# A pre-norm attention and LoRA block on one core: key parts written straight into their rows, x of the second chunk by tiles, the first layer norm in halves, 22 turns ahead of the first tile

## The chip, the cores and the metric

The kernel runs on 1 core of one Trainium2 chip. The metric is the device time of one execution in microseconds. Before the change the median of 3 runs is 701.74 us (701.54 to 702.16).

## What is computed

The input x has 2 x 1024 tokens of 512 numbers, all in float32. A block of attention is followed by a feed-forward block, each behind a layer norm without weights and each added back:

```python
x = x + attn(layernorm(x), Wqkv, Wo)     # 32 heads of 16, one key and value head shared by all, causal, ALiBi
x = x + ffn(layernorm(x), W_base, b_base, W_gate, A, B)   # x @ W_base.T + b + routed LoRA, top 2 of 8 experts
# attn: scores = q @ k.T * scale + slopes * (pos_k - pos_q), causal, softmax, @ v, heads joined, @ Wo
```

## The kernel before, in words

**Stages.** The tokens are four chunks of 512 (`c` = 0 to 3, two per batch). Ahead of the attention, chunk by chunk: SP loads x, VectorE makes the layer norm's statistics (`statistics`) and, with a first guess of the inverse deviation from ScalarE (`rstd_first`) and one Newton step, the normed x (`normalised`). TensorE turns it by 128x128 pieces (`turn_tile`, L663), ScalarE copies the turned tile out of PSUM (`copy_tile`, L887), and TensorE projects in float32 to queries (four groups of 128 columns) and to one group of 112 columns: six copies of the 16 key columns, and the values (`project`, L678).

**Parts.** The scores are made in bf16 matmuls from operands that hold a float32 number as a sum of bf16 parts: high, middle, low. Six products of parts are added by one matmul, since each stands in 16 rows of its own: `PARTS` says for each 16 rows which part of q and which of k stand there. For queries ScalarE makes the float32 copy and the high part (L899, L907), VectorE (queries 0 and 1) or POOL (the others) the rest, and SP writes the parts to DRAM (`store_queries`) and reads them back row group by row group (`load_queries`, six transfers). For keys ScalarE copies the group of 112 rows to `kv` (`keys_values`, L915); VectorE's `split_keys` makes the parts of all 96 rows in seven instructions (L1102 to L1114), the last three of which mask each part by a column of 0 and 1 and add them into `k_op`.

**Attention.** A step k handles one unit of 4 heads x 2 chunks of queries. Its maxima go one step ahead of its scores: TensorE fills a PSUM bank (`max_slot`, L732), VectorE takes the maximum out of it (L1145 on the diagonal, L1150 beside it): 40 such slots and 2 turns of the results per step, in three banks. Then come the scores (L759, L762), their exponentials by ScalarE (L965), and the product with the values (L780). 16 steps are followed by the output projection (L808) and the feed-forward block.

**Order.** Each engine runs a fixed list. TensorE's is made by `pe_order`: scores and values of the step before, slots of this step, and projections put among them (`AMONG`). A slot goes in where `slot_due` says, which spreads the slots by VectorE's time as `vector_time` guesses it: so many ns a slot, and 620 ns more for a slot that has a piece of `split_keys` behind it (`KEY_SLOTS`: seven slots in steps 0, 2 and 4, one for each piece). In step 0, chunk 1's keys are split behind slots 2 to 8; slots 16 on read `q_in[1]`, the second chunk's queries.

**What the change touches:** `PARTS`, `KEY_SLOTS` and `vector_time`; on SP the load of chunk 1's x (L455); on TensorE the start (L855); on ScalarE `rstd_first` (L878) and `keys_values` (L909); on VectorE `statistics` (L1068), `normalised` (L1083), `split_keys` (L1098) and the first calls (L1157).

## Time and profile before

| what | value |
|---|---|
| median of 3 runs | 701.74 us |
| the profiled execution's own time | 700.96 us |
| its span, first to last instruction | 699.2 us |
| TensorE busy (matmul) | 669.7 us, 96% |
| VectorE busy | 557.4 us, 80% |
| ScalarE busy | 358.6 us, 51% |
| POOL busy | 216.9 us, 31% |
| TensorE's share of the chain that ended last | 83% |

TensorE's busy time is close to the span, so what can be gained without less matmul work is the 29.5 us in which it stands still. A table by stretches shows where these lie.

### The profile page before, as it was taken

Reading aid. Unit: us, or ns where it says so; the run is one execution under the profiler, and the core shown is the slowest. Engines: PE = TensorE matmul, PEld = TensorE weight load, DVE = VectorE, ACT = ScalarE, POOL = GpSimd, SP = SyncE. Lnnn points to the kernel's source line nnn. Section 1 sums busy time; section 2 is a strip of 40 time slices with the busy share of each in tenths; the row PEclk is TensorE's granted clock in tenths of the full one; section 3 lists DMA queues with packets and bytes.
Section 4 is the critical chain, followed back from the end, with each engine's and each line's share of the span. In section 5 each row is a group of like instructions: output and inputs, shape, how many; then the busy total and the mean of one; then the engine's idle time right before and its main releaser. Section 6 shows DMA issues by size and latency. Waiting matters only on the chain.

```text
span 699.2 us, 13261 instructions
## 1 busy us (share of the span) xinstructions
PE 669.7 (96%) x4304; PEld 305.5 (44%) x4304; DVE 557.4 (80%) x1801; ACT 358.6 (51%) x511; POOL 216.9 (31%) x366
## 2 busy tenths in 40 slices
PE   3889999999999999999999999999999999999997
PEld 2434344544344444444443343433433455555553
DVE  5899889887989889898988989899881365666565
ACT  2324647567556676666666666767667411111111
POOL 0035424233332515243352231422432412222220
PEclk9999999999999999999999999999999999999999
DMA  8578108080411443080144744225200189700001
GB/s 253 130 145 137 64 2 136 30 147 28 166 54 51 60 89 108 11 131 34 41 63 94 102 81 77 49 49 94 48 18 33 52 130 170 162 30 30 31 30 60
DMA packets 42951, 56.32 MB, mean 81 GB/s; under 512 B 6648, under 2 KB 26232, under 8 KB 42752
## 3 DMA queue, kind: packets, MB, share of 16 engines
q1 hardware_dynamic: 40296, 51.27, 37.3%
q10 hardware_dynamic: 2592, 4.26, 1.8%
q8 instruction: 33, 0.54, 0.3%
q14 instruction: 30, 0.25, 0.1%
HBM read 35.72 MB, written 19.79 MB: 79 GB/s over the span
## 4 chain that ended last, share of the span: by engine, by line
PE 83%; DVE 10%; DMA 3%; ACT 2%; issue 1%; SPq 1%; POOL 0%; DVEq 0%; ACTq 0%; POOLq 0%
PE psum L780 20%; PE psum L732 18%; PE psum L762 13%; PE psum L808 8%; PE psum L830 7%; PE psum L678 7%; PE psum L759 5%; DVE psum L1145 3%; PE psum L825 2%; PE psum L840 2%; ACT work L965 2%; DMA x_sb<-in_x 1%; DVE negm L1150 1%; PE psum L817 1%; DMA arena<-q_dram 1%
## 5 line engine op out<-in xcount | busy, mean ns | idle before, releaser
L965 ACT ACTIVATE work<-psum 128x1024 f32<-128x1024 f32 (+1 forms) x320 | 289.0, 943 | 127.6 <-PE psum L762 108.5
L1145 DVE CUSTOM_DVE_ANT_0 psum<-psum,future 128x384 f32<-128x384 f32 (+3 forms) x512 | 237.7, 514 | 12.6 <-PE psum L732 10.4
L732 PE MATMUL psum<-k_op,arena 106*128 106x512 bf16 (+3 forms) x768 | 212.4, 328 | 9.6 <-DVE negm L1145 4.3
L1150 DVE TENSOR_REDUCE negm<-psum 128x1 f32<-128x512 f32 x256 | 168.6, 687 | 15.3 <-PE psum L732 10.9
L1318 POOL TENSOR_SCALAR_AFFINE_SELECT work<-work 128x512 f32<-128x512 f32 x128 | 81.2, 634 | 296.2 <-ACT work L965 296.2
L780 PE MATMUL psum<-work,v_op 128*32 128x512 f32 (+3 forms) x1536 | 163.5, 498 | 0.5 <-POOL work L1318 0.4
L762 PE MATMUL psum<-arena,k_op 109*128 109x512 bf16 (+3 forms) x640 | 157.3, 316 | 1.9 <-ACT work L965 0.8
L732 PEld LDWEIGHTS psum<-k_op,arena 106*128 106x128 bf16 x768 | 69.0, 97 | 128.5 <-DVE negm L1145 40.7
L678 PE MATMUL psum<-arena,wqkv_sb 128*128 128x256 f32 (+3 forms) x240 | 84.6, 453 | 1.1 <-ACT arena L887 1.1
L759 PE MATMUL psum<-arena,k_op 116*128 116x128 bf16 x512 | 84.3, 221 | 0.9 <-ACT work L965 0.9
L762 PEld LDWEIGHTS psum<-arena,k_op 109*128 109x128 bf16 x640 | 59.6, 98 | 44.5 <-ACT work L965 15.7
L1145 DVE DVE_READ_ACCUMULATOR2_ANT negm<- 128x1 f32 x512 | 70.0, 137 | 0.0
L759 PEld LDWEIGHTS psum<-arena,k_op 116*128 116x128 bf16 x512 | 44.4, 98 | 48.4 <-ACT work L965 36.1
L808 PE MATMUL psum<-wo_sb,wqkv_sb 128*128 128x512 f32 x128 | 59.0, 596 | 0.4 <-issue 0.4
L830 PE MATMUL psum<-wb_sb,x_sb 128*128 128x512 f32 x128 | 57.5, 593 | 0.0
L780 PEld LDWEIGHTS psum<-work,v_op 128*32 128x32 f32 x1536 | 30.5, 108 | 51.0 <-issue 40.8
L678 PEld LDWEIGHTS psum<-arena,wqkv_sb 128*128 128x128 f32 (+1 forms) x240 | 43.5, 188 | 20.7 <-issue 10.8
L1348 POOL TENSOR_TENSOR x_sb<-x_sb,bias_sb 128x512 f32<-128x512 f32 x16 | 20.3, 1266 | 100.6 <-DVE wqkv_sb L1242 100.6
L899 ACT ACTIVATE arena<-psum 128x256 f32<-128x256 f32 (+1 forms) x24 | 10.9, 454 | 61.0 <-PE psum L678 57.2
L830 PEld LDWEIGHTS psum<-wb_sb,x_sb 128*128 128x128 f32 x128 | 23.2, 190 | 22.9 <-issue 22.9
L808 PEld LDWEIGHTS psum<-wo_sb,wqkv_sb 128*128 128x128 f32 x128 | 22.7, 191 | 23.2 <-issue 23.2
L1197 DVE TENSOR_TENSOR x_sb<-work,psum 128x512 f32<-128x512 f32 x12 | 8.3, 688 | 28.9 <-PE psum L808 28.8
(86 smaller groups left out, 454.8 us busy)
## 6 DMA issues: line engine op xcount, KB each, us to landing
arena<-q_dram SPq DMA_DIRECT2D x96, 128.0 KB, 5.5
o_dram<-o_sb SPq DMA_DIRECT2D x32, 256.0 KB
q_dram<-arena SPq DMA_DIRECT2D x16, 384.0 KB, 4.4
arena<-o_dram SPq DMA_DIRECT2D x32, 128.0 KB, 4.6
arena<-rcp_dram SPq DMA_DIRECT2D x32, 128.0 KB, 4.9
out<-wqkv_sb ACTq DMA_DIRECT2D x16, 256.0 KB, 2.0
x_sb<-in_x SPq DMA_DIRECT2D x3, 1024.0 KB, 10.0
work<-in_x SPq DMA_DIRECT2D x3, 1024.0 KB, 18.8
```

Source lines behind the costliest of these rows:

```text
L678: last = nc.tensor.matmul(psum[0:width, bank, 0:n], wqkv_sb[:, part, first:first + width], xnT[:, c % 2, part, columns], start=(part == 0) ...
L732: last = nc.tensor.matmul(bank[:, a * width:(a + 1) * width], q_op[0:ROW_MAX, bass.ds(col, P)], k_op[0:ROW_MAX, b, k0:k0 + width], start=T ...
L759: last = nc.tensor.matmul(at[:, 0:P], k_op[0:STAIR_ROWS, b, t * P:(t + 1) * P], q_op[0:STAIR_ROWS, bass.ds(col, P)], start=True, stop=True)
L762: last = nc.tensor.matmul(at[:, diag:w], k_op[0:ROWS, b, t * P:(t + 1) * P], q_op[0:ROWS, bass.ds(col + diag, w - diag)], start=True, stop ...
L780: last = nc.tensor.matmul(psum[VW * j:VW * (j + 1), 7, off:CH], v_op[:, b * (S // P) + t, m % 2, :], probs[:, n % 4, j, 0:CH - off], start ...
L808: last = nc.tensor.matmul(psum[:, n % 2], att[:, n % 2, g, :], wo_sb[:, g, :], start=(g == 0), stop=(g == PAIRS - 1))
L830: nc.tensor.matmul(psum[:, 6 + n % 2], xn2T[:, n % 2, k, :], wb_sb[:, k, :], start=(k == 0), stop=False)
L965: nc.scalar.activation(probs[:, n % 4, heads * hp:heads * (hp + 1), 0:w], src, ACT.Exp).then_inc(exp_done, 1)
L1145: last = nc.vector.tensor_tensor_reduce(keys, keys, future[:, CH - width:CH], -1.0, 3e38, ALU.add, ALU.min, negm[:, late, 0, j * QT + t:j ...
L1150: nc.vector.tensor_reduce(dst, psum[:, bank, 0:len(js) * width].rearrange("p (a k) -> p a k", a=len(js)), AX_X, ALU.max, negate=True).then ...
L1318: nc.gpsimd.affine_select(out=d, in_=d, compare_op=ALU.is_ge, fill=0.0, base=0, pattern=[[0, UH], [1, P]], channel_multiplier=-1).then_inc ...
L1348: nc.gpsimd.tensor_tensor(out=x1b[:, n % 2], in0=x1[:, n % 2], in1=bias_sb[:], op=ALU.add).then_inc(x1b_ready, 1)
```

## The change

**Parts.** The order of `PARTS` is such that key rows 0 to 31 and 80 to 95 hold the high part, 32 to 63 the middle, 64 to 79 the low. ScalarE, behind its copy to `kv`, copies all 96 rows from PSUM into `k_op` as bf16 as well, which is the high part in all rows. VectorE subtracts it from `kv` (96 rows), rounds the rest (96 rows), copies the middle part over rows 32 to 63, and writes the low part to rows 64 to 79: four instructions for seven, without masks. `KEY_SLOTS` has four slots for seven in steps 0, 2 and 4, at 530 ns for 620.

**Start.** Chunk 1's x comes by four loads of one tile for one load of four, and its statistics wait tile by tile. Chunk 0's layer norm is made in halves of two tiles: statistics of both, then normed. TensorE makes 22 turns of the identity matrix into a PSUM bank before the first tile.

The diff, cut to its core:

```diff
--- before.py
+++ after.py
@@ -46,7 +46,9 @@
 NU = 2 * NK
-PARTS = ((0, 0), (0, 1), (0, 2), (1, 0), (1, 1), (2, 0))
+PARTS = ((0, 0), (1, 0), (0, 1), (1, 1), (0, 2), (2, 0))
+MID_KEYS = slice(2 * DH, 4 * DH)
+LOW_KEYS = slice(4 * DH, 5 * DH)
 ROW_ALIBI = len(PARTS) * DH
@@ -63,6 +65,7 @@
 NT = B * S // P
+WARMING = 22
 LINKS_PER_TILE = 16
@@ -157,7 +160,7 @@
-KEY_SLOTS = {0: range(2, 9), 2: range(3, 28, 4), 4: range(3, 28, 4)}
+KEY_SLOTS = {0: range(2, 6), 2: range(3, 16, 4), 4: range(3, 16, 4)}
 STAT_SLOTS = (3, 5, 7, 9)
@@ -168,7 +171,7 @@
     if r in KEY_SLOTS.get(k, ()):
-        time += 620
+        time += 530
     if k == 1 and r in STAT_SLOTS:
@@ -332,8 +335,7 @@
         k_rest = k_tmp[0:96, CH:2 * CH]
-        k_sum = k_tmp[0:96, 2 * CH:3 * CH]
-        k_part = k_tmp[0:96, 3 * CH:3 * CH + 3 * CH // 2].bitcast(BF16).rearrange("p (a q) -> p a q", a=3)
+        k_mid = k_tmp[0:96, 2 * CH:2 * CH + CH // 2].bitcast(BF16)
         stats = sb("stats", [P, QT, 6])
@@ -368,6 +370,7 @@
         x0_in = [sem(f"x0_in{t}") for t in range(QT)]
+        x1_in = [sem(f"x1_in{t}") for t in range(QT)]
         x_in = [sem(f"x_in{c}") for c in range(NCH)]
@@ -452,7 +455,8 @@
                 sp.dma_start(wqkv_sb[:, k], wqkv[P * k:P * (k + 1)]).then_inc(w_in, 16)
-            sp.dma_start(x_sb[:, 1], x_rows[1]).then_inc(x_in[1], 16)
+            for t in range(QT):
+                sp.dma_start(x_sb[:, 1, t], x_rows[1][:, t]).then_inc(x1_in[t], 16)
@@ -853,6 +857,8 @@
             pe.wait_ge(ident_in_sem, 16)
+            for _ in range(WARMING):
+                nc.tensor.transpose(psum[:, 0, 0:P], ident[:], ident[:])
             for u, use in enumerate(BEFORE):
@@ -875,12 +881,13 @@
         def _(act):
-            def rstd_first(c):
-
-                act.wait_ge(var_ready, c + 1)
-                nc.scalar.activation(lnv[:], ve[:], ACT.Ln).then_inc(ln_done, 1)
-                act.wait_ge(ln_done, c + 1)
-                nc.scalar.activation(rstd[:], lnv[:], ACT.Exp, scale=-0.5).then_inc(rstd_guess, 1)
+            def rstd_first(c, some=slice(0, QT)):
+
+                n = c + 1 if c or some.start else 0
+                act.wait_ge(var_ready, n + 1)
+                nc.scalar.activation(lnv[:, some], ve[:, some], ACT.Ln).then_inc(ln_done, 1)
+                act.wait_ge(ln_done, n + 1)
+                nc.scalar.activation(rstd[:, some], lnv[:, some], ACT.Exp, scale=-0.5).then_inc(rstd_guess, 1)
@@ -912,7 +919,10 @@
                     act.wait_ge(side_full, VALUES[c - 1])
-                nc.scalar.copy(kv[:, columns], psum[0:112, USE_AT[u][0], 0:CH if half is None else CH // 2]).then_inc(side_free, 1)
+                found = psum[0:112, USE_AT[u][0], 0:CH if half is None else CH // 2]
+                nc.scalar.copy(kv[:, columns], found)
+                first = (c % 2) * CH + columns.start
+                nc.scalar.copy(k_op[0:96, c // 2, first:(c % 2) * CH + columns.stop], found[0:96]).then_inc(side_free, 1)
@@ -938,7 +948,8 @@
             act.preload_act_table_set("natural_log_exp_and_others")
-            rstd_first(0)
+            rstd_first(0, slice(0, 2))
+            rstd_first(0, slice(2, QT))
             for u, use in enumerate(BEFORE):
@@ -1067,8 +1078,8 @@
                 for t in tiles:
-                    if c == 0:
-                        dve.wait_ge(x0_in[t], 16)
+                    if c == 1:
+                        dve.wait_ge(x1_in[t], 16)
                     elif t == 0:
@@ -1080,10 +1091,30 @@
+            def half_statistics(some):
+
+                for t in range(some.start, some.stop):
+                    dve.wait_ge(x0_in[t], 16)
+                    last = nc.vector.bn_stats(stats[:, t], x_sb[:, 0, t])
+                link(last)
+                for t in range(some.start, some.stop):
+                    last = nc.vector.bn_aggr(mv[:, t], stats[:, t])
+                link(last)
+                nc.vector.tensor_scalar(ve[:, some], mv[:, some, 1], EPS, None, ALU.add).then_inc(var_ready, 1)
+
+            def half_normalised(some):
+                n = 1 if some.start == 0 else 2
+                dve.wait_ge(rstd_guess, n)
+                dve.wait_ge(var_ready, n)
+                newton(rstd[:, some], ve[:, some], newt[:, some])
+                for t in range(some.start, some.stop):
+                    nc.vector.tensor_scalar(x_sb[:, 0, t], x_sb[:, 0, t], mv[:, t, 0:1], rstd[:, t:t + 1],
+                                            ALU.subtract, ALU.mult).then_inc(xn_ready, 1)
+
             def normalised(c, tiles):
                 if tiles[0] == 0:
-                    dve.wait_ge(rstd_guess, c + 1)
-                    dve.wait_ge(var_ready, c + 1)
+                    dve.wait_ge(rstd_guess, c + 2)
+                    dve.wait_ge(var_ready, c + 2)
                     newton(rstd[:], ve[:], newt[:])
@@ -1097,24 +1128,18 @@
+                keys = k_op[:, c // 2, (c % 2) * CH:(c % 2 + 1) * CH]
                 if piece == 0:
                     dve.wait_ge(side_free, use_count("kv", c, None, 1 if c >= 2 else None))
-                    link(nc.vector.tensor_copy(k_part[:, 0], kv[0:96]))
+                    link(nc.vector.tensor_tensor(k_rest[:], kv[0:96], keys[0:96], ALU.subtract))
                 elif piece == 1:
-                    link(nc.vector.tensor_tensor(k_rest[:], kv[0:96], k_part[:, 0], ALU.subtract))
+                    link(nc.vector.tensor_copy(k_mid[:], k_rest[:]))
                 elif piece == 2:
-                    link(nc.vector.tensor_copy(k_part[:, 1], k_rest[:]))
-                elif piece == 3:
-                    link(nc.vector.tensor_tensor(k_part[:, 2], k_rest[:], k_part[:, 1], ALU.subtract))
-                elif piece == 4:
-                    link(nc.vector.tensor_scalar(k_sum[:], k_part[:, 0], kmask[0:96, 0:1], None, ALU.mult))
-                elif piece == 5:
-                    link(nc.vector.scalar_tensor_tensor(k_sum[:], k_part[:, 1], kmask[0:96, 1:2], k_sum[:], ALU.mult, ALU.add))
+                    nc.vector.tensor_copy(keys[MID_KEYS], k_mid[MID_KEYS])
                 else:
-                    nc.vector.scalar_tensor_tensor(k_op[0:96, c // 2, (c % 2) * CH:(c % 2 + 1) * CH], k_part[:, 2],
-                                                   kmask[0:96, 2:3], k_sum[:], ALU.mult, ALU.add).then_inc(k_ready, 1)
-
-            KEY_PIECES = 7
+                    nc.vector.tensor_tensor(keys[LOW_KEYS], k_rest[LOW_KEYS], k_mid[LOW_KEYS], ALU.subtract).then_inc(k_ready, 1)
+
+            KEY_PIECES = 4
@@ -1154,8 +1179,10 @@
-            statistics(0)
-            normalised(0, range(QT))
+            half_statistics(slice(0, 2))
+            half_statistics(slice(2, QT))
+            half_normalised(slice(0, 2))
+            half_normalised(slice(2, QT))
             statistics(1)
```

The table of slots moves instructions on TensorE. In step 0, between the slots of the diagonal (L1145's) and the first slot that reads the second chunk's queries, its rows were these before (L678 is a projection, L732 a slot; `q_in1` stands for the second chunk's queries, `k_ready` for the keys, `slot_free` for a bank that VectorE has emptied):

```order
L678 MATMUL psum<-arena,wqkv_sb 128x512
L732 MATMUL psum<-k_op,arena 128x384 [waits slot_free]
L678 MATMUL psum<-arena,wqkv_sb 128x512 [waits side_free]
L732 MATMUL psum<-k_op,arena 128x512 [waits slot_free]
L678 MATMUL psum<-arena,wqkv_sb 128x512
L732 MATMUL psum<-k_op,arena 128x512 [waits slot_free]
L678 MATMUL psum<-arena,wqkv_sb 128x512
L732 MATMUL psum<-k_op,arena 128x512 [waits slot_free] x2
L678 MATMUL psum<-arena,wqkv_sb 128x512
L732 MATMUL psum<-k_op,arena 128x512 [waits q_in1,k_ready,slot_free]
```

And now, in the changed kernel (whose line numbers are 4 higher here):

```order
L682 MATMUL psum<-arena,wqkv_sb 128x512
L736 MATMUL psum<-k_op,arena 128x384 [waits slot_free]
L736 MATMUL psum<-k_op,arena 128x512 [waits slot_free]
L682 MATMUL psum<-arena,wqkv_sb 128x512 [waits side_free]
L736 MATMUL psum<-k_op,arena 128x512 [waits slot_free] x2
L682 MATMUL psum<-arena,wqkv_sb 128x512
L736 MATMUL psum<-k_op,arena 128x512 [waits slot_free]
L682 MATMUL psum<-arena,wqkv_sb 128x512
L736 MATMUL psum<-k_op,arena 128x512 [waits q_in1,k_ready,slot_free]
```

Four projections stand in this piece where there were five: the slots moved ahead, and one projection lies behind the slot that waits for `q_in1`.

On VectorE, in the same place (L1145 is a slot's maximum; ISA is its custom instruction), the pieces of the keys stood among the slots like this before:

```order
L1106 CAST k_tmp<-k_tmp 96x512
L1145 ISA psum,negm<-psum,future 128x384
L1108 TENSOR_TENSOR k_tmp<-k_tmp 96x512
L1110 TENSOR_SCALAR k_tmp<-k_tmp,kmask 96x512
L1112 SCALAR_TENSOR_TENSOR k_tmp<-k_tmp,kmask 96x512
L1145 ISA psum,negm<-psum,future 128x512
L1114 SCALAR_TENSOR_TENSOR k_op<-k_tmp,kmask 96x512
```

And now:

```order
L1134 TENSOR_TENSOR k_tmp<-k_tmp,k_op 96x512
L1136 CAST k_tmp<-k_tmp 96x512
L1170 ISA psum,negm<-psum,future 128x384
L1138 COPY k_op<-k_tmp 32x512
L1140 TENSOR_TENSOR k_op<-k_tmp 16x512
```

The keys are complete behind the second of the four slots of 384 columns; before they were behind the first of the four of 512 columns.

## Rows read from the trace of the kernel before

**Rows 1.** The page: busy time by engine, and TensorE's granted clock in 40 slices.

```profile
PE 669.7 (96%) x4304; PEld 305.5 (44%) x4304; DVE 557.4 (80%) x1801; ACT 358.6 (51%) x511; POOL 216.9 (31%) x366
...
PEclk9999999999999999999999999999999999999999
```

**Rows 2.** Busy time by stretches, all engines (the last three: clock, DMA share, GB/s).

```profile
32.30:67.00 34.70, 32.24 (x122) 15.37 (x122) 32.24 (x98) 8.59 (x17) 14.15 (x17) 1.00 0.77 137
67.00:100.00 33.00, 29.90 (x211) 12.79 (x211) 30.45 (x100) 19.63 (x26) 10.30 (x20) 1.00 0.19 51
165.00:200.00 35.00, 33.61 (x255) 14.96 (x253) 31.17 (x95) 21.31 (x29) 11.81 (x21) 1.00 0.27 89
```

**Rows 3.** The chain that ended last, up to 33 us (start, us, what).

```profile
4.66 9.95 DMA x_sb<-in_x
...
21.84 2.53 DMA q_dram<-arena
...
26.67 5.51 DMA arena<-q_dram
```

**Rows 4.** VectorE in order of time, the first layer norm (start, us, instruction).

```profile
8.53 0.16 DVE L1063 TENSOR_TENSOR newt<-rstd 128x4 f32<-128x4 f32 x1 [0.51 <-ACT rstd L883]
...
9.33 1.92 DVE L1089 TENSOR_SCALAR x_sb<-x_sb,mv,rstd 128x512 f32<-128x512 f32 x4
```

**Rows 5.** TensorE in order of time, up to 24 us.

```profile
10.02 3.65 PE L663 MATMUL psum<-ident,x_sb 128*128 128x128 f32 x16 [10.02 <-DVE x_sb L1089]
14.34 7.13 PE L678 MATMUL psum<-arena,wqkv_sb 128*128 128x512 f32 x16 [0.67 <-ACT arena L887]
21.31 2.19 PE L663 MATMUL psum<-ident,x_sb 128*128 128x128 f32 x16
```

**Rows 6.** ScalarE in order of time, 18 to 32 us.

```profile
18.72 0.62 ACT L907 CAST arena<-arena 128x512 bf16<-128x512 f32 x1
21.51 0.59 ACT L915 COPY k_tmp<-psum 112x512 f32<-112x512 f32 x1 [2.18 <-PE psum L678]
22.00 2.17 ACT L887 COPY arena<-psum 128x512 f32<-128x512 f32 x4
...
28.64 0.62 ACT L907 CAST arena<-arena 128x512 bf16<-128x512 f32 x1
```

**Rows 7.** SP's queue in order of time.

```profile
24.39 2.71 SPq L500 DMA_DIRECT2D arena<-q_dram  x6
31.86 0.38 SPq L485 DMA_DIRECT2D q_dram<-arena  x1
34.72 2.67 SPq L500 DMA_DIRECT2D arena<-q_dram  x6
```

**Rows 8.** TensorE at 32 us, the first slots.

```profile
32.32 0.60 PE L732 MATMUL psum<-k_op,arena 106*128 106x128 bf16 x6 [0.91 <-DMA arena<-q_dram]
```

**Rows 9.** TensorE at 42 to 45 us, up to the first slot that reads `q_in[1]`.

```profile
42.30 0.39 PE L732 MATMUL psum<-k_op,arena 106*128 106x512 bf16 x1 [0.74 <-DVE negm L1145]
...
44.42 0.39 PE L732 MATMUL psum<-k_op,arena 106*128 106x512 bf16 x1 [0.88 <-DVE negm L1145]
```

**Rows 10.** The keys' pieces, by tile (ns min/median/max, first and last start).

```profile
L1102 DVE CAST k_tmp<-k_tmp x4: 411/414/419, 22.6 to 170.9; 96x512 bf16<-96x512 f32 x4
L1104 DVE TENSOR_TENSOR k_tmp<-k_tmp x4: 681/682/689, 23.1 to 173.6; 96x512 f32<-96x512 f32 x4
...
L1108 DVE TENSOR_TENSOR k_tmp<-k_tmp x4: 669/685/1435, 24.3 to 179.6; 96x512 bf16<-96x512 f32 x4
...
L1112 DVE SCALAR_TENSOR_TENSOR k_tmp<-k_tmp,kmask x4: 743/746/1041, 25.5 to 186.7; 96x512 f32<-96x512 bf16 x4
L1114 DVE SCALAR_TENSOR_TENSOR k_op<-k_tmp,kmask x4: 739/744/1600, 26.3 to 190.2; 96x512 bf16<-96x512 bf16 x4
```

**Rows 11.** VectorE's smallest copy, the turned maxima, by line.

```profile
L1134 DVE COPY m_t<-psum x32: 268/278/280, 48.6 to 523.5; 16x128 f32<-16x128 f32 x32
```

**Rows 12.** TensorE at 182 us, in step 4.

```profile
181.80 0.29 PE L732 MATMUL psum<-k_op,arena 106*128 106x128 bf16 x2 [0.85 <-DVE negm L1150]
```

## The prediction

> **What bounds the kernel now.** I read the page first. TensorE's matmuls cover 96% of the span, VectorE's work 80% [rows 1], so the matmul time of 669.7 us, which this change doesn't touch, stands, and a gain has to come out of TensorE's 29.5 us of standing still. The second view is the table by stretches [rows 2]. It shows that the two engines share the lead only at the front: from 32.3 to 67 us (step 0) both are busy for 32.24 of 34.70 us, TensorE standing still for 2.5; from 67 to 100 us (step 1) TensorE stands still for 3.1 us and from 165 to 200 us (step 4) for 1.4. Ahead of 32.3 us lies the third part: TensorE's first instruction comes at 10.02 us [rows 5]. The third view is the chain of waits [rows 3]: up to step 0 it goes through the load of chunk 1's x (4.66 to 14.61 us), its layer norm, the store of queries 0 (21.84) and their load back (to 32.18), to the first slot at 32.32 us [rows 8]. I then read each engine in order of time along that chain.
>
> **The first tiles.** The halves take VectorE's wait of 0.51 us for ScalarE's guess away, since the second half's statistics fill it, and make Newton's four steps twice. These steps run from 8.53 to 9.33 us [rows 4], so 0.8 us. Norming a tile takes 1.92/4 = 0.48 us [rows 4]. The first tile is then normed at 8.0 + 0.8 + 0.5 = 9.3 us where it was 9.8, the fourth at 8.0 + 2 x 0.8 + 4 x 0.48 = 11.5 where it was 11.25. So the halves help the first tile and hurt the last, and alone would be worth nothing.
>
> What makes the gain is the 22 turns. The 16 turns of chunk 0 take 3.65 us, 228 ns each, those of chunk 1 2.19 us, 137 ns each [rows 5]: the same instruction on the same shapes. The page's granted clock is at full speed in the first slices too [rows 1], but it can't say more than its first record, and the turns are what tell: the first 16 ran slow, as at 1.2 GHz, and the projection behind them at full speed (7.13/16 = 0.446 us for each record, [rows 5]). So 3.65 us of turns were there before the clock rose. 22 turns at 228 ns are 5.0 us; the identity matrix is asked for in the first microsecond, and they should lie between some 4 and 9 us, hidden behind the layer norm (if they ended 0.5 us later, that 0.5 would be lost). I take chunk 0's turns at 0.55 us a tile. The fourth tile is turned at 11.5 + 0.1 + 0.55 = 12.1 us where it was 13.67: 1.5 us earlier.
>
> The Trainium skill has a rule against this ("TensorE: Matmul & The Clock Gate", Part 4: PE-mode transpose): the clock doesn't rise for transposes, which don't count as busy in the same way. By the trace it rose behind nothing but turns [rows 5]; by that rule the 22 turns would buy nothing, which is a rival below.
>
> **The second chunk's turns.** The first projections end 1.5 us earlier, at 19.95 us for 21.47 [rows 5]. Behind them ScalarE now has two copies for one. The copy to `kv` takes 0.59 us and the four tiles' copies 2.17 us [rows 6]; the new copy into `k_op` (96 rows of 512 from PSUM, to bf16) has no row of its own and lies between 0.59 and the 0.62 of L907 [rows 6]; I take 0.6. So the last tile is out at 19.95 + 0.59 + 0.6 + 2.17 = 23.3 us for 24.17, and the second projections start and end only 0.85 us earlier: at 30.55 us for 31.41. ScalarE takes half of the gain back here.
>
> **Slot 0.** It needs queries 0 back from DRAM. Their store went out at 21.84 us [rows 3], held by the layer norm of chunk 1's x. With statistics tile by tile three of the four (2.48 us, so 1.86) are done before the last tile lands, if that one lands no earlier than now; the store then goes at 20.0 us. The high part of queries 0, at 19.34 us now [rows 6], comes at 17.85, and VectorE's three pieces (0.68 + 0.41 + 0.68 and gaps, [rows 10]) end at 19.8: about the same. Four loads for one cost SP two or three issues more, which delay constants that nobody reads before slot 0. The loads back end 1.8 us earlier, at 30.35 us. So slot 0 starts at 30.6 us, behind the projections, for 32.32: 1.7 us.
>
> **Step 0.** The keys' seven pieces cost VectorE some 5.3 us in this step: two casts of 0.41, two subtractions of 0.68, a masking that I put between them at 0.5, and the last two, of which these are the longest times, 1.04 and 1.60 [rows 10]. Now it is 0.68 + 0.41 + 0.68 and one copy of 32 rows, bf16 to bf16, which no row shows. It lies between 0.28 [rows 11] and the cast's 0.41 [rows 10]; I take 0.3, since it writes half the bytes. Together 2.1 us, 3.2 us less. TensorE's waits of 0.74 and 0.88 us for VectorE [rows 9] go with that.
>
> What is late next is the first slot that reads `q_in[1]`, at 44.42 us now [rows 9]. Three things must be there. TensorE: 12.1 us from slot 0 to it, less 0.74 + 0.88, less one projection that now lies behind it (7.13/8 = 0.87), gives 9.6, so 40.2 us. VectorE: 44.42 - 1.7 - 3.2 = 39.5 us. Queries 1: their high part was ready at 29.26 us [rows 6] and comes at 28.4; three pieces, store at 30.3 us for 31.86; then 2.86 us to the first load back (34.72 - 31.86, [rows 7]), and from the first load to the last landing 7.8 us, as for queries 0 (24.39 to 32.18, [rows 3, 7]): 41.0 us. So **a new wait for a load** of about 0.9 us takes the place of the waits for VectorE. TensorE and VectorE both stand; behind it everything on TensorE's list is queued. The slot starts at 41.1 us, 3.3 us earlier, with 0.87 us of projection still owed: step 0 ends **2.45 us** earlier. From there TensorE has work without gaps, as it had.
>
> **Later steps.** Step 1 has no key pieces, its own 3.1 us stay. Its chunk-2 keys, and chunk 3's in step 3, add two half copies on ScalarE each, behind an exponential. They lie between half of 0.59 us and 0.59 [rows 6]. ScalarE is 51% busy [rows 1], and the halves of queries in later steps already put a copy and a cast at the same kind of place, so I cost them at nothing. Uncovered they would be 4 x 0.4 = 1.6 us, and the forecast's 698.6 would be 700.2, inside the range. In steps 2 and 4 VectorE has 2 us less or more. TensorE waited 0.85 us at 181.80 us for it [rows 12], behind L1108, which took 1435 ns for 685 beside POOL [rows 10]; a short instruction now stands there, but of the same kind. I take half of step 4's 1.4 us: **0.7 us**, between 0 and 1.4. Nothing behind step 4 changes.
>
> **The sum.** 2.45 + 0.7 = 3.15 us off the profiled execution's 700.96 us gives 697.8. The median of the runs shown, 701.74, lies 0.8 above that execution, so **698.6 us**.
>
> **The rivals.** (1) The clock doesn't rise for the 22 turns. Chunk 0's turns take 3.65 us from 9.3 on, ending at 12.95 for 12.1, and all that rests on the first projections comes 0.85 us later: gain 2.3, so 699.4 us. Against it stand rows 5. (2) The queries are not late, and VectorE's lead holds into step 1: the loads back took 7.8 us beside traffic that may have moved. Then 0.9 us more in step 0, a fifth of step 1's 3.1, and the other 0.5 of step 4: 5.2 us, 696.5 us. For it: VectorE's lead of 3.2 us has to be spent somewhere. (3) Queries 1 come back as late as now, since their way is a chain of transfers and only its start moved; at 42.5 us (34.72 + 7.8) the slot is at 42.6, 0.95 us less after the projection owed, and step 4 gives nothing: 700.8 us, no change that can be measured. (4) The table that places slots is wrong for the new pieces. TensorE runs its list in order, so a slot that comes before VectorE has emptied its bank stops the scores behind it, and ScalarE's exponentials and POOL's masks after them. That is how step 1 runs, 3.1 us in 33 [rows 2]. If steps 2 and 4, both rebuilt, ran like that, step 4 would lose 1.7 us and step 2 up to 3.1: 4.8 against 2.45 gained, 704.1 us. It decides from 2.45 us of new waits on. Against it: VectorE has less work in both, not more. That the change doesn't do what it says is not among these: the order of instructions shows it.
>
> **How the numbers follow.** The forecast has 0.56, rival 1 0.12, rival 2 0.17, rival 3 0.10, rival 4 0.05. About 0.2% (1.4 us) is what a measurement of this kernel can tell from no change. Forecast, rivals 1 and 2 are faster by more: 0.85; rival 3 is the same: 0.10; rival 4 slower: 0.05. The range goes from rival 2 to just short of rival 3, 696.4 to 700.6 us, which takes in the unknown copies' bounds and leaves out some 2 in 10.
>
> **What would show it.** Right: chunk 0's turns in 2.2 to 2.5 us in place of 3.65; the first slot at 30 to 31 us; no wait for VectorE above 0.5 us at 35 to 41 us, and one of 0.5 to 1.5 us for `arena<-q_dram` ahead of the slot that reads `q_in[1]`; from step 5 on each step as long as before. Wrong: turns at 228 ns; no wait for the load; TensorE idle over 2 us in a stretch like that of step 2 or 4; or a first slot later than 31.5 us.

## The result, and the profile after

The changed kernel takes 698.46 us (median of 6 runs, 697.74 to 699.74); the kernel before, on the same chip, 701.95 us (701.54 to 702.82). The ratio is 0.9947, with an interval of 0.9930 to 0.9964: 3.5 us faster. The profiled execution took 698.62 us with a span of 696.9 us, 2.3 us less than the span before. In this section gains are differences between the two profiled executions. One later execution of the kernel before (766.93 us, mean granted clock 0.853) is left out of every ratio and range below.

The page of the changed kernel, the rows that answer to [rows 1]:

```profile
PE 673.5 (97%) x4326; PEld 308.8 (44%) x4326; DVE 552.3 (79%) x1794; ACT 360.7 (52%) x519; POOL 216.5 (31%) x366
```

TensorE has 22 instructions more and stands still for 23.4 us where it was 29.5. But 4.96 us of that difference are the 22 turns, which are no work. VectorE lost 5.1 us of work and ScalarE gained 2.1.

**The start.** TensorE in order of time, up to slot 0 (start, us, instruction, count, in brackets the idle time before it and what ended it), beside [rows 5, 8]:

```profile
3.92 4.96 PE L861 MATMUL psum<-ident 128*128 128x128 f32 x22 [3.92 <-DMA ident<-in_ident]
9.07 1.45 PE L667 MATMUL psum<-ident,x_sb 128*128 128x128 f32 x8 [0.19 <-DVE x_sb L1111]
10.77 1.11 PE L667 MATMUL psum<-ident,x_sb 128*128 128x128 f32 x8 [0.25 <-DVE x_sb L1111]
12.59 7.13 PE L682 MATMUL psum<-arena,wqkv_sb 128*128 128x512 f32 x16 [0.71 <-ACT arena L894]
...
22.91 7.11 PE L682 MATMUL psum<-arena,wqkv_sb 128*128 128x512 f32 x16 [0.46 <-ACT arena L894]
31.44 0.60 PE L736 MATMUL psum<-k_op,arena 106*128 106x128 bf16 x6 [1.42 <-DMA arena<-q_dram]
```

The 22 turns end 0.19 us before the first tile is there, at 4.96/22 = 225 ns each, the duration at the lower level of the clock. The second eight turns of chunk 0 take 139 ns each, the duration at the higher one. The first projections start 1.75 us earlier and the second 1.39 us, ending at 30.02 us. Slot 0 starts only 0.88 us earlier. What holds it is in its brackets: 1.42 us of standing still for the load of queries 0.

VectorE in order of time, the statistics of chunk 1's x, of which the last tile arrives late:

```profile
11.08 1.28 DVE L1085 BATCH_NORM_STATS2 stats<-x_sb 128x6 f32<-128x512 f32 x2
12.53 0.69 DVE L1085 BATCH_NORM_STATS2 stats<-x_sb 128x6 f32<-128x512 f32 x1 [0.17 <-DMA x_sb<-in_x]
14.97 0.69 DVE L1085 BATCH_NORM_STATS2 stats<-x_sb 128x6 f32<-128x512 f32 x1 [1.75 <-DMA x_sb<-in_x]
```

Three tiles are done by 13.2 us; the fourth lands at 14.95, 0.3 us later than the single load did [rows 3]. So VectorE stands still for 1.75 us. The changed kernel's SP queue, in order of time, carries the rest of the chain:

```profile
20.41 0.38 SPq L489 DMA_DIRECT2D q_dram<-arena  x1
23.12 2.70 SPq L504 DMA_DIRECT2D arena<-q_dram  x6
29.81 0.38 SPq L489 DMA_DIRECT2D q_dram<-arena  x1
32.35 3.65 SPq L504 DMA_DIRECT2D arena<-q_dram  x6
```

Queries 0 are stored 1.43 us earlier than before, but the way from the store to the last landing takes 10.9 us (20.41 to 31.3) where it took 10.3 (21.84 to 32.18). The transfers gave 0.55 us of the early store back.

**Step 0.** TensorE around the first slot that reads `q_in[1]`, which before waited 0.88 us [rows 9]:

```profile
38.59 0.93 PE L736 MATMUL psum<-k_op,arena 106*128 106x512 bf16 x2 [0.17 <-DVE negm L1170]
39.35 1.02 PE L682 MATMUL psum<-arena,wqkv_sb 128*128 128x512 f32 x2
40.22 0.38 PE L736 MATMUL psum<-k_op,arena 106*128 106x512 bf16 x1
40.44 1.02 PE L682 MATMUL psum<-arena,wqkv_sb 128*128 128x512 f32 x2
41.30 0.60 PE L736 MATMUL psum<-k_op,arena 106*128 106x512 bf16 x2
```

The row at 41.30 is that slot. Nothing stands in brackets: the load of queries 1 landed at 40.12 us, 1.2 us ahead of it, and of the waits for VectorE of [rows 9] 0.17 us is left. VectorE's key pieces by tile (ns min/median/max, first and last start, forms), beside [rows 10]:

```profile
L1134 DVE TENSOR_TENSOR k_tmp<-k_tmp,k_op x4: 673/678/685, 21.2 to 169.0; 96x512 f32<-96x512 f32 x4
L1136 DVE CAST k_tmp<-k_tmp x4: 418/418/422, 21.9 to 171.8; 96x512 bf16<-96x512 f32 x4
L1138 DVE COPY k_op<-k_tmp x4: 283/284/349, 22.4 to 175.3; 32x512 bf16<-32x512 bf16 x4
L1140 DVE TENSOR_TENSOR k_op<-k_tmp x4: 683/789/1503, 22.7 to 178.3; 16x512 bf16<-16x512 f32 x4
```

The copy of 32 rows takes 0.28 us. The last piece, with 16 rows, costs as much as one with 96 rows (683 ns at the least), and up to 1503.

**Steps 2 and 4.** The stretches of step 0, 1, 2 and 4 in the changed kernel (from:to, length, then busy time of TensorE, its weight loads, VectorE, ScalarE, POOL, clock, DMA share, GB/s), beside [rows 2]:

```profile
31.40:64.10 32.70, 32.08 (x122) 15.46 (x122) 30.34 (x95) 8.56 (x17) 13.60 (x17) 1.00 0.78 143
64.10:97.10 33.00, 30.03 (x211) 12.71 (x211) 30.40 (x100) 20.21 (x28) 10.34 (x20) 1.00 0.15 47
97.10:131.30 34.20, 33.10 (x259) 16.39 (x262) 28.94 (x87) 22.29 (x31) 11.50 (x21) 1.00 0.49 84
163.00:198.00 35.00, 33.77 (x259) 15.46 (x261) 29.42 (x92) 21.75 (x30) 11.87 (x22) 1.00 0.27 89
```

And step 2 in the kernel before:

```profile
100.00:134.20 34.20, 33.90 (x266) 16.65 (x266) 29.36 (x90) 23.04 (x32) 12.47 (x23) 1.00 0.50 85
```

In step 2 TensorE stands still for 1.1 us (34.20 - 33.10) where it was 0.3, though VectorE has less to do. The place in the changed kernel's trace:

```profile
110.19 1.16 POOL L1310 TENSOR_TENSOR arena<-arena 128x512 bf16<-128x512 f32 x1
110.39 1.50 DVE L1140 TENSOR_TENSOR k_op<-k_tmp 16x512 bf16<-16x512 f32 x1
...
112.67 0.28 PE L736 MATMUL psum<-k_op,arena 106*128 106x128 bf16 x2 [0.64 <-DVE negm L1175]
```

The last key piece runs beside a subtraction on POOL and takes 1.50 us for 0.68; behind it TensorE waits 0.64 us for a maximum. In step 4 the same two instructions overlap for 0.35 us only, and the piece takes 0.90 us:

```profile
177.47 1.16 POOL L1310 TENSOR_TENSOR arena<-arena 128x512 bf16<-128x512 f32 x1
178.28 0.90 DVE L1140 TENSOR_TENSOR k_op<-k_tmp 16x512 bf16<-16x512 f32 x1
```

Both pieces end 0.54 us behind the end of POOL's subtraction.

The gain along the program, taken at the end of each step (the turn of its last maxima; 66.58 us in the kernel before is that of step 0): 2.89 us behind step 0, 2.90 behind step 1, **1.98 behind step 2**, 1.98 behind step 3, 2.32 behind step 4, and 2.34 at the end.

### The profile page after: what moved, and what is told of

It is laid out like the page before. It is cut to its first block, busy times and chain, and to the rows that moved or that the text cites. A ratio compares the mean times of both kernels' runs of the same rounds, so it can differ in the third digit from the quotient of the medians.

```text
span 696.9 us, 13297 instructions
## 1 busy us (share of the span) xinstructions
PE 673.5 (97%) x4326; PEld 308.8 (44%) x4326; DVE 552.3 (79%) x1794; ACT 360.7 (52%) x519; POOL 216.5 (31%) x366
## 4 chain that ended last, share of the span: by engine, by line
PE 83%; DVE 9%; DMA 2%; ACT 2%; issue 1%; SPq 1%; POOL 0%; DVEq 0%; ACTq 0%; POOLq 0%
PE psum L784 20%; PE psum L736 18%; PE psum L766 13%; PE psum L812 8%; PE psum L834 7%; PE psum L682 7%; PE psum L763 5%; DVE psum L1170 3%; PE psum L829 2%; PE psum L844 2%; ACT work L976 2%; DVE negm L1175 1%; DMA x_sb<-in_x 1%; PE psum L821 1%; DMA arena<-q_dram 1%
## 5 line engine op out<-in xcount | busy, mean ns | idle before, releaser
L682 PEld LDWEIGHTS psum<-arena,wqkv_sb 128*128 128x128 f32 (+1 forms) x240 | 43.4, 188 | 20.4 <-issue 10.2
L906 ACT ACTIVATE arena<-psum 128x256 f32<-128x256 f32 (+1 forms) x24 | 10.9, 454 | 59.6 <-PE psum L682 59.6
L812 PEld LDWEIGHTS psum<-wo_sb,wqkv_sb 128*128 128x128 f32 x128 | 22.7, 190 | 23.2 <-issue 23.2
L1224 DVE TENSOR_TENSOR x_sb<-work,psum 128x512 f32<-128x512 f32 x12 | 8.2, 687 | 29.4 <-PE psum L812 29.4
```

The lines of the kernel that those rows point to most:

```text
L682: last = nc.tensor.matmul(psum[0:width, bank, 0:n], wqkv_sb[:, part, first:first + width], xnT[:, c % 2, part, columns], start=(part == 0) ...
L812: last = nc.tensor.matmul(psum[:, n % 2], att[:, n % 2, g, :], wo_sb[:, g, :], start=(g == 0), stop=(g == PAIRS - 1))
```

## The experiments

Each kernel is the changed one with the edit shown (cut to its core), and its ratio is to the kernel before, timed beside it. "Step" is the time from one step's last maxima to the next's; step 11 shows whether the clock fell ahead of it.

| kernel | median us | ratio to before (interval) | span | slot 0 at | step 2 | step 4 | step 11 |
|---|---|---|---|---|---|---|---|
| before | 701.95 to 702.87 | 1 | 699.2 | 32.32 | 33.25 | 32.90 | 29.42 |
| the change | 698.46 | 0.9947 (0.9930 to 0.9964) | 696.9 | 31.44 | 34.16 | 32.56 | 29.42 |
| r1_after | 699.60 | 0.9953 (0.9936 to 0.9970) | 697.2 | 31.77 | 34.17 | 32.56 | 29.42 |
| e1_no_warm | 700.39 | 0.9957 (0.9943 to 0.9971) | 700.7 | 33.24 | 34.16 | 32.56 | 30.60 |
| e2_keys_only | 701.45 | 0.9990 (0.9974 to 1.0006) | 701.4 | 33.76 | 34.17 | 32.56 | 30.60 |
| e3_start_only | 699.86 | 0.9959 (0.9935 to 0.9983) | 697.7 | 31.23 | 33.24 | 32.90 | 29.42 |
| e4_one_x_load | 701.79 | 0.9959 (0.9937 to 0.9980) | 702.9 | 35.27 | 34.16 | 32.56 | 30.7 |
| e10_whole_ln | 699.26 | 0.9955 (0.9938 to 0.9973) | 698.3 | 31.46 | 34.17 | 32.56 | 30.60 |
| e5_pieces | 700.26 | 0.9962 (0.9946 to 0.9978) | 699.6 | 31.74 | 34.40 | 33.50 | 30.63 |
| e6_recip | 700.90 | 0.9977 (0.9959 to 0.9994) | 699.1 | 32.19 | 34.40 | 33.50 | 27.77 |
| e7_const | 701.42 | 0.9977 (0.9965 to 0.9990) | 700.1 | 32.42 | 34.40 | 33.51 | 29.42 |
| e8_plan | 697.90 | 0.9936 (0.9922 to 0.9951) | 696.1 | 32.17 | 33.13 | 32.10 | 29.42 |
| e9_both | 697.73 | 0.9934 (0.9918 to 0.9950) | no use | | | | |
| e11_both_again | 695.52 | 0.9903 (0.9880 to 0.9925) | 694.0 | 31.16 | 33.13 | 32.09 | 27.77 |

The kernel before was timed again beside every group of kernels; its median moved by 0.9 us from group to group, so ratios are compared, not medians. The profiled execution of e9_both took 2847 us, with slot 0 at 127.75 us, while its other runs took 695.11 to 699.14: that profile says nothing on the kernel, and why it happened is open. Differences between profiled executions in slot 0 and in step 11 are in part those of one execution; I say where.

**The changed kernel again.**

> The changed kernel as it is, run beside the next three as their reference. Theory A (the granted clock of the first 30 us differs from run to run, and the 22 turns bring its rise in front of the projections every time): in this profile too the clock has risen by 10.5 us and chunk 0's turns take 2.2 to 2.6 us; its times lie within 2.5 us of each other while those of the kernel before spread over 4 to 5 us. Theory B (the profile of 698.62 us was a lucky one): the clock rises later than 12 us or falls again before 30 us, and the times spread as widely as those of the kernel before.

The gain behind each step is 2.58, 2.58, 1.66, 1.66 and 2.01 us for steps 0 to 4: the loss of 0.92 us in step 2 and the 0.35 us regained in step 4 repeat to a hundredth. The medians' ratio repeats the result. The clock rises at 8.2 us, as expected; that the times would lie closer together than those of the kernel before did not come true (697.79 to 701.74 us here, 699.97 to 704.24 there).

Slot 0 varies. Six profiles have the same front (the change, r1, e5, e6, e8, e11), and their slot 0 lies between 31.16 and 32.19 us. In all six, and in e3 and e10, the store of queries 0 goes out 5.45 to 5.46 us behind the landing of the fourth tile of chunk 1's x, which comes at 14.78 to 15.97 us. So that landing sets the store, and slot 0 follows 10.6 to 11.0 us behind the store. A difference of under 1 us in slot 0 between two of these profiles says little about their kernels. From slot 0 to the end of step 0 the six take 32.23 to 32.31 us, the kernel before 34.26: this part of the gain, 2.0 us, repeats.

**Without the 22 turns.**

```diff
-WARMING = 22
+WARMING = 0
```

> The changed kernel without the 22 turns. Theory A (the clock rose for the 22 turns, but slot 0 hangs on the last tile of chunk 1's x, its layer norm and the way of queries 0 through DRAM): chunk 0's turns go back to some 228 ns each, the first projections start about 0.8 us later than 12.59 us, and slot 0 still comes at 31.4 to 31.7 us, so the whole is at most 0.3 us slower. Theory B (TensorE's list sets slot 0): slot 0 comes 0.8 us later and so does the end. By the clock rule of the Trainium skill (TensorE: Matmul & The Clock Gate, Part 4) the turns would not change at all.

TensorE in order of time without them:

```profile
9.49 3.65 PE L667 MATMUL psum<-ident,x_sb 128*128 128x128 f32 x16 [9.49 <-DVE x_sb L1111]
13.81 9.29 PE L682 MATMUL psum<-arena,wqkv_sb 128*128 128x512 f32 x16 [0.68 <-ACT arena L894]
```

The turns go back to 228 ns each, and the slow stretch now reaches into the first projections: 9.29 us for 7.13. Slot 0 is 1.8 us later than in the changed kernel, at 33.24, later than before the change too, and by more than either theory had. Keys alone (below) shows the same slow stretch, 9.02 us. The trace's granted clock rises to 2.4 GHz at 18.2 and 18.4 us in these two, at 13.7 in the profile of the kernel before, and between 6.7 and 9.8 us in the ten usable profiles of kernels with the 22 turns. In all ten the first projections take 7.13 us. So the turns buy more than the 0.85 us that I gave them where the rise would have been late, and they take that spread of the first projections away. The medians' ratios (0.9957 without, 0.9947 and 0.9953 with) differ by 0.3 to 0.7 us, less than their intervals: the medians alone don't show that the turns gain anything.

**The keys alone, and the start alone.** e2 has the key parts with the old start: no turns, one load of chunk 1's x, a whole layer norm. e3 has the start, with the old `PARTS`, `KEY_SLOTS` and `split_keys`, and ScalarE's one copy.

```diff
-WARMING = 22
+WARMING = 0
...
-            for t in range(QT):
-                sp.dma_start(x_sb[:, 1, t], x_rows[1][:, t]).then_inc(x1_in[t], 16)
+            sp.dma_start(x_sb[:, 1], x_rows[1]).then_inc(x1_in[0], 16)
```

> The new split of the keys and its slots alone, on the start of the kernel before. Theory A (the gain of step 0 is VectorE's): slot 0 at 32.2 to 32.5 us; step 0 ends 1 to 1.9 us earlier than before (late turn 65.6 to 64.7 us for 66.6); step 2 loses up to 0.9 us where the last piece stands beside POOL, step 4 gives 0.3; the whole 1 to 1.4 us faster than before. Theory B (the new copy of ScalarE delays queries 1, which then come late): a wait of 0.5 to 1 us for a load ahead of the first slot that reads them, and under 1 us gained in step 0.

```diff
-KEY_SLOTS = {0: range(2, 6), 2: range(3, 16, 4), 4: range(3, 16, 4)}
+KEY_SLOTS = {0: range(2, 9), 2: range(3, 28, 4), 4: range(3, 28, 4)}
...
-        time += 530
+        time += 620
```

> The new start alone (22 turns, layer norm in halves, x by tiles) with the keys of the kernel before. Theory A (the parts add up): slot 0 at 31.3 to 31.5 us for 32.32, the 0.9 us stay to the end, whole 0.9 us faster than before. Theory B (VectorE sets step 0, so an early start is spent waiting for it): gain at the end of step 0 under 0.4 us.

The start alone gains 1.51 us at the end of step 0 and keeps it to the end (1.54). TensorE's waits for VectorE are still in step 0 of e3, in order of time:

```profile
40.78 0.39 PE L737 MATMUL psum<-k_op,arena 106*128 106x512 bf16 x1 [0.74 <-DVE negm L1175]
...
42.91 0.39 PE L737 MATMUL psum<-k_op,arena 106*128 106x512 bf16 x1 [0.87 <-DVE negm L1175]
```

The whole change gains 2.89 us there, so the key parts are worth 1.4 us in step 0 (1.6 if each is counted from its own slot 0: 33.85 us in e3, 32.25 in the changed kernel). They lose 0.92 in step 2: e2 and the changed kernel have 34.16 us where e3 and the kernel before have 33.25. They gain 0.34 in step 4 and end at +0.8. The medians agree in order: 0.9959 for the start, 0.9990 for the keys, an interval that holds no change. For the keys both theories missed the start: slot 0 came at 33.76 us, not at 32.2 to 32.5, with the late rise of the clock told above, and step 0 ended 0.36 us later than before the change, though counted from slot 0 it was 1.1 us shorter. The wait that I predicted for queries 1 exists in e2, where slot 0 follows the second projections without waiting for a load:

```profile
44.55 0.59 PE L735 MATMUL psum<-k_op,arena 106*128 106x512 bf16 x2 [0.58 <-DMA arena<-q_dram]
```

**One load of chunk 1's x, and a whole layer norm.** e4 undoes the loads by tile; e10 the halves.

```diff
-                        dve.wait_ge(x1_in[t], 16)
+                        if t == 0:
+                            dve.wait_ge(x1_in[0], 16)
```

> The changed kernel with chunk 1's x in one load of 1 MB again. Theory A (statistics of three tiles ahead of the last landing are what moved slot 0): landing at 14.6 us, queries 0 stored 0.9 to 1.5 us later than 20.41 us, slot 0 at 32.3 to 32.9 us, whole 0.9 to 1.4 us slower than the changed kernel. Theory B (the last tile's landing at 14.95 us is late because there are four loads): landing near 13 us and nothing lost.

```diff
-            half_statistics(slice(0, 2))
-            half_statistics(slice(2, QT))
-            half_normalised(slice(0, 2))
-            half_normalised(slice(2, QT))
+            statistics(0)
+            normalised(0, range(QT))
```

> The changed kernel with chunk 0's layer norm in one piece again. Theory A (the halves help the first tile and hurt the last, which is what the projections wait for): first turn at 9.8 to 10.0 us, first projections within 0.3 us of 12.6 to 12.8, slot 0 unchanged. Theory B (the halves are needed: with them the pause between the 22 turns and the first tile is short and the clock stays up): a pause over 1 us, turns of chunk 0 at the slow rate or a clock that rises after 12 us, first projections 0.8 us or more later.

With one load TensorE waits for the second chunk, and the clock falls. Two rows of TensorE, and a stretch of e4's table by stretches with its clock (the third number from the end):

```profile
23.98 1.94 PE L666 MATMUL psum<-ident,x_sb 128*128 128x128 f32 x8 [1.62 <-DVE x_sb L1120]
...
26.68 7.90 PE L681 MATMUL psum<-arena,wqkv_sb 128*128 128x512 f32 x14
```

```profile
24.00:29.00 5.00, 4.98 (x15) 3.49 (x16) 4.85 (x11) 1.50 (x4) 0.00 (x0) 0.50 0.47 132
```

The trace's granted clock falls at 23.2 us, in the second of two waits (0.98 and 1.62 us), and stands at 1.2 GHz until 30.0; slot 0 comes at 35.27 us. The single load landed at 16.16 us, later than either theory had (15.96 in e2, 14.61 in the kernel before). With one load the store of queries 0 goes out 7.2 to 7.4 us behind the landing in these three, for the 5.46 of the loads by tile: the 1.8 us by which three tiles' statistics come early are real. The 6.0 us of span that this profile loses are not what the median loses: its ratio, 0.9959, is within the interval of the changed kernel, so what the loads by tile are worth in most executions the medians can't tell. The whole layer norm leaves slot 0 where it was (31.46 for 31.44): the first tile comes at 9.97 us for 9.07, but the first projections only 0.18 us later (12.77; TensorE stood still for 1.22 us ahead of that tile, and the clock stayed up), and the store of queries 0 hangs on the fourth tile's landing in both. The halves are worth nothing that these runs can show, as their sum in the prediction said.

**The pieces elsewhere in steps 2 and 4.** Two theories for the lost 0.92 us: the last piece collides with POOL's subtraction, or the table of slots spreads the slots wrongly. e5 leaves TensorE's list as it is (`KEY_SLOTS` feeds the planner) and moves only VectorE's pieces.

```diff
+PIECE_SLOTS = {2: range(2, 12, 3), 4: range(2, 12, 3)}
...
-                    if r in KEY_SLOTS.get(k, ()):
-                        split_keys(k // 2 + 1, KEY_SLOTS[k].index(r))
+                    if r in PIECE_SLOTS.get(k, ()):
+                        split_keys(k // 2 + 1, PIECE_SLOTS[k].index(r))
```

> The changed kernel with the keys' pieces of steps 2 and 4 behind slots 2, 5, 8, 11 of VectorE's list for 3, 7, 11, 15; TensorE's list stays. Theory A (the loss of 0.9 us in step 2 is the last piece's 1.50 us beside POOL's subtraction): the piece takes 0.68 us in both steps, the gap of 0.64 us at 112.7 us is gone, and step 2's late turn comes 0.6 to 0.9 us earlier against step 1's; step 4 gains up to 0.4; whole 0.7 to 1.2 us faster than the changed kernel. Theory B (it is the new order of slots on TensorE): a gap of 0.5 us or more stays in step 2.

In step 2 the last piece is back to 0.68 us and no wait of TensorE is above 0.30 us, and the step takes 34.40 us all the same, a little more than in the changed kernel: neither theory holds as it was put. In step 4 the collision, 0.35 us long in the changed kernel, becomes a whole one:

```profile
176.12 1.16 POOL L1307 TENSOR_TENSOR arena<-arena 128x512 f32<-128x512 f32 x1
176.28 1.54 DVE L1141 TENSOR_TENSOR k_op<-k_tmp 16x512 bf16<-16x512 f32 x1
```

and that step grows from 32.56 to 33.50 us, with a wait of 1.04 us on TensorE at 178.6 us. So the collision is real and its price is seen, but without it step 2 is no shorter: the collision alone isn't the cause there.

**The old plan of slots with the new pieces.** e8 gives the planner the seven marks of 620 ns back in steps 2 and 4, and puts the four new pieces at four of them.

```diff
-KEY_SLOTS = {0: range(2, 6), 2: range(3, 16, 4), 4: range(3, 16, 4)}
+KEY_SLOTS = {0: range(2, 6), 2: range(3, 28, 4), 4: range(3, 28, 4)}
+PIECE_SLOTS = {2: (3, 7, 11, 19), 4: (3, 7, 11, 19)}
...
-        time += 530
+        time += 530 if k == 0 else 620
```

> The changed kernel with the order of TensorE's list in steps 2 and 4 as in the kernel before (seven key slots at 620 ns in the plan), and the four pieces behind slots 3, 7, 11, 19. Theory A (the 0.92 us that step 2 lost come from the plan: with less time set aside for keys, slots are due at other places, and one stands where VectorE has not emptied its bank): step 2 takes 33.2 to 33.3 us between its late turns for 34.17, step 4 32.6 to 32.9; whole 0.6 to 1.0 us faster than the changed kernel. Theory B (it is the last piece beside POOL): step 2 is as long as in e5_pieces or the changed kernel unless the piece itself takes 0.68 us, and then by that much shorter.

Step 2 takes 33.13 us and step 4 32.10, 1.03 and 0.46 less than in the changed kernel, and both less than before. The last piece is at one duration in all four chunks:

```profile
L1141 DVE TENSOR_TENSOR k_op<-k_tmp x4: 683/683/683, 23.6 to 180.4; 16x512 bf16<-16x512 f32 x4
```

e5 had moved the pieces under the new plan and gained nothing; under the old plan, at other places, they gain. That speaks for the plan as a part of the cause. But e8 moved both the plan and the fourth piece, and the new plan with the fourth piece behind slot 19 was not run: how much of the 1.03 us is the plan's, and that it has a part at all, is argued and not shown.

**Constants later.** On top of e5, the constants are issued behind the load of chunk 2's x, to let the fourth tile land early.

```diff
-            load_constants(0)
             def load_x(c):
...
             load_x(2)
+            load_constants(0)
```

> The kernel of e5_pieces with the constants that nobody reads before slot 0 (qalibi, stair, kalibi, future) issued behind the load of chunk 2's x for ahead of it. Theory A (the last tile of chunk 1's x lands at 14.95 us, 2.4 us behind the third, because constants run beside it): it lands at 12.7 to 13.3 us, the store of queries 0 goes out at 19.8 us for 20.41, held by ScalarE's high part, and slot 0 comes 0.5 to 0.8 us earlier. Theory B (the last tile's way is slow by itself): landing over 14.3 us and slot 0 as before, or later by what the constants lose.

The fourth tile landed at 12.94 us for 14.95, and queries 0 were stored at 20.13. But the constants then ran beside the store. SP's queue in order of time:

```profile
20.13 0.40 SPq L485 DMA_DIRECT2D q_dram<-arena  x1
24.69 2.69 SPq L500 DMA_DIRECT2D arena<-q_dram  x6
```

The store took 4.56 us for 2.71, and slot 0 came at 32.42, 0.7 us later than in e5 and 0.2 later than in e6 and e8, which have e5's front. The fourth tile landed at 14.1 to 16.0 us in the nine profiles with the constants behind it on the queue, so the constants do hold it; moved there, they stand beside the store. In this execution the clock also fell from 34.0 to 37.4 us.

**Reciprocals in quarters.** In step 10 VectorE inverts the sums of the first batch in one piece of 1.73 us (L1180), and TensorE waits 1.32 us behind it in the changed kernel; step 11 is as long in both. e6 takes it in four pieces (on top of e5); e9 and e11 are one kernel, e8 with the quarters four slots later.

```diff
+            RECIP_SLOTS = (27, 30, 33, 36)
+            def reciprocal_quarter(b, q):
+                if q == 0:
+                    dve.wait_ge(sums_in, 16 * (b + 1))
+                part = sums[:, q * P // 2:(q + 1) * P // 2]
+                made = nc.vector.reciprocal(part, part)
...
-                step(k)
-                if k == NB + 2:
-                    reciprocals(0)
+                for r in range(NSL):
+                    step(k, None, (r,))
+                    if k == NB + 2 and r in RECIP_SLOTS:
+                        reciprocal_quarter(0, RECIP_SLOTS.index(r))
```

> The kernel of e5_pieces with the reciprocals of the first batch in four quarters behind slots 27, 30, 33, 36 of step 10, for one instruction of 1.73 us behind its last slot. Theory A (TensorE stands still for 1.3 us at 382 us because VectorE does nothing else for it in 1.73 us, and that pause is where the clock can fall): the gap goes, the late turn of step 11 comes 1.2 us earlier against step 10's, no fall of the clock there, whole 1.2 us faster than e5_pieces and up to 2.4 where that one's clock falls. Theory B (VectorE has no room among the slots of step 10 either): the late turn of step 10 comes 1 to 1.7 us later and nothing is gained.

> The kernel of e8_plan with the reciprocals in quarters behind slots 31, 34, 37, 40 of step 10, when the sums have landed. Theory A (in e6_recip it was the wait of 1.25 us for the sums that cost step 10 its time): steps 10 and 11 together take 56.2 to 56.7 us for 57.19 in the changed kernel, step 11 27.8. Theory B (VectorE's 1.73 us have no room in step 10): together 57.2 to 57.6 as in e6_recip. If A holds this is the fastest version: 1.2 to 2 us faster than the changed kernel.

> The kernel of e9_both once more, for a profile of an undisturbed execution (the profiled one of e9_both took 2847 us, with TensorE slow throughout). The same theories: A, steps 10 and 11 together 56.2 to 56.7 us for 57.19, step 11 27.8, no fall of the clock behind step 10; B, together 57.2 to 57.6. By the times of e9_both (695.11 to 699.14 us in its undisturbed runs) A gives a median of 696.5 to 698 us.

VectorE's first quarter in e6:

```profile
373.78 0.55 DVE L1189 RECIPROCAL sums<-sums 128x64 f32<-128x64 f32 x1 [1.25 <-DMA sums<-sum_dram]
```

The place was too early: the sums were not back, VectorE stood for 1.25 us, and step 10 grew by 2.02 us while step 11 shrank by 1.65. Four slots later (e11) step 10 takes 28.29 us and step 11 27.77, together 56.06 for 57.19: 1.13 us gained. e11 has a span of 694.0 us, and at 695.52 us (694.51 to 696.72), ratio 0.9903 (0.9880 to 0.9925), it beats both kernels. e9, the same kernel, had 0.9934 (0.9918 to 0.9950). The two intervals just overlap, so 0.7 to 1.0% is what I would claim. e9 was timed beside e8 and differed from it by nothing that can be measured (697.73, 697.90), so the medians don't confirm the 1.13 us by themselves; the traces do. Of the 12 usable executions of e9 and e11 one has a mean granted clock of 0.998 or less, as the profiles with a fall of the clock have; of the 23 of the kernel before that were timed beside them it is 10. The kernel of e6, whose quarters stand earlier, has 4 in 11.

## Why the prediction was right

The median lies 0.1 us from the predicted 698.6, inside the range, and the change is faster, as forecast. That it is so close is luck. In step 0 two errors partly cancel: up to slot 0 the gain was 0.88 us for 1.7, behind it 2.0 for 0.75. Steps 2 and 4 went the other way than forecast. What made up for them is that the profile of before, from which the sum starts, was a fast one. Two of the prediction's own signs of being wrong came true: no wait for the load of queries 1 and, in four of the six profiles with this front, a first slot later than 31.5 us.

**The first tiles** were right: the last turned at 11.88 us for the predicted 12.1, the turns in 1.45 + 1.11 = 2.56 us for the 2.2 to 2.5 named. Rival 1 fell. The clock rises behind nothing but turns of the identity matrix, and e1 shows what is lost without them. The Trainium skill says the reverse ("TensorE: Matmul & The Clock Gate", Part 4: PE-mode transpose): by that rule the 22 turns would do nothing. The traces don't agree, for these float32 turns: in all ten profiles with them the clock had risen by 9.8 us, behind nothing but turns. What I mis-sized is their worth. I took the profile of before for typical, but its clock rose at 13.7 us, and two of the three profiles without turns show 18.2 and 18.4.

**The second chunk's turns.** ScalarE's extra copy took 0.58 us where I said 0.6, but that it takes back half of the gain didn't hold to the same amount: the second projections start 1.39 us earlier for 0.85 predicted, at 22.91. The first projections ended 0.2 us sooner than reckoned, and the three rows of ScalarE's copies overlap (19.76, 20.24 and 20.72 us), which the sum of their durations left out. In the five other profiles with this front the second projections start at 23.36 to 23.89 us, so most of what this profile has above 0.85 us is its own.

**Slot 0** is a term that failed: 31.44 us for 30.6, outside the 30 to 31 us named as a sign of being right. Three steps of it: the fourth tile of x landed at 14.95 us for the 14.6 taken, so the store of queries 0 went at 20.41 for 20.0; the store took 2.7 us for 2.5; and the loads back took 8.2 us for 7.8. All are transfers, which I took at one profile's time and let move with the start. The fourth tile's landing alone varies by 1.2 us (14.78 to 15.97), and slot 0 with it.

**Step 0.** The pieces cost what was said (0.68, 0.42, 0.28, 0.68 for the predicted 0.68, 0.41, 0.3, 0.68) and the waits for VectorE went. The predicted new wait of 0.9 us for queries 1 **did not come**. They landed at 40.12 us for the predicted 41.0, since their store went at 29.81 for 30.3 and the way back took 10.3 us for 10.7. The slot came at 41.30, 9.9 us behind slot 0 for the 9.6 reckoned; with slot 0 at the predicted 30.6 it would have come at 40.5, still behind the landing. The other five profiles with this front have no such wait either, with the landing 0.1 to 0.9 us ahead of the slot. So step 0 gained 2.89 us for 2.45. The wait is real in e2, which has 0.58 us of it: there queries 1 landed at 44.42 us.

**Steps 2 and 4** were wrong in sign: 0.7 us of gain forecast, 0.92 - 0.34 = 0.6 us of loss measured. The step that failed is the overlap in step 2: I looked only at VectorE having less work, and named rival 4's mechanism in its full size of 4.8 us, for which I gave 0.05. It holds in small. In step 2 the last piece fell beside POOL's subtraction, cost 1.50 us for 0.68 and left TensorE waiting 0.64 us; the old plan with another place for that piece gave the loss back, and how the two share it stays open. The wait of [rows 12] did shrink, from 0.85 us to 0.39 (at 179.95 us), as I had argued for step 4, though another grew (0.51 us at 170.3, for 0.25 at 172.1 before); step 2, without such a wait before, had nothing to give and much to lose.

**Rivals 2 and 3.** Rival 2's 0.9 us more in step 0 came about by half (2.89 for 2.45), without the rest, since step 1 kept its 3.0 us. Rival 3 is excluded by the landing at 40.12. By the predicted sum, 2.45 + 0.7 = 3.15; by the trace, 2.89 - 0.58 = 2.3, 0.8 less. That the median is nonetheless 3.5 us lower fits the profile of before, whose 700.96 us lie 1.0 below the median of 701.95. Falls of the clock don't account for that: in the later groups 37 of the 66 other executions of the kernel before have a mean granted clock above 0.998, and their median is 702.28 us, with 8 at 700.96 or less. What was shorter in that execution, the early rise of its clock or the landing of x at 14.61 us, is argued and not shown.

## What to carry to other kernels

A change that makes one engine's work shorter has to be followed through the plan made for the old work: the old table of slots, with the four new pieces placed in it, was worth 1.5 us in steps 2 and 4 together, more than half of what the whole change showed in the trace. When a start is moved, write out which transfer ends last behind it; here 1.75 us won at the first projections became 0.88 at slot 0. One profile says when the clock rose once, and when a load landed once: compare several before pricing anything that depends on them.

## What the runs showed of the hardware

- The rise of TensorE's clock varies: 13.7, 18.2 and 18.4 us in the profiles without early work, with the same first turn at 9.5 to 10.2 us; 6.7 to 9.8 us in the ten with 22 turns from 3.9 to 4.1 us on.
- It can fall again. In five of the profiles (e1, e2, e4, e5, e10) it fell between 384 and 389 us, for 3.4 us, behind TensorE's wait of 1.3 us for the reciprocals; in the others that have this wait (before, the change, r1, e3, e7, e8) it didn't fall there. Step 11 then took 30.6 us for 29.4. Here e2's two stretches (columns as above):

```profile
386.00:388.00 2.00, 1.46 (x11) 0.40 (x12) 2.00 (x13) 0.35 (x1) 0.46 (x2) 0.75 0.07 14
388.00:390.00 2.00, 2.00 (x11) 1.18 (x9) 1.53 (x8) 0.82 (x1) 0.00 (x0) 0.50 0.01 0
```

- A subtraction on VectorE that started while POOL ran one (both with all operands in SBUF) ended 0.54 to 0.55 us behind the end of POOL's, in all 23 cases that the thirteen usable profiles have in the splitting of keys: it took 0.75 to 1.54 us, by how much of POOL's was left (0.20 to 1.00 us). With nothing on POOL it took 0.67 to 0.69 us, on 16 rows as on 128, and beside POOL's mask (L1346 in e5, at 108.2 us) 0.68.
- The store of queries 0 (384 KB) took 2.5 to 2.9 us in eleven profiles, 3.4 in e4, and 4.5 us in e7, where the constants were issued ahead of it.
- In eight profiles the store of queries 0 went out 5.45 to 5.46 us behind the landing of x's last tile, which itself lay between 14.78 and 15.97 us.
